# Time mixing with gate and layer norm on eight cores: unlinked transfers in the head, first products of k's mixes on ScalarE

## The chip, the cores and the metric

One Trainium2 chip, eight cores, one launch. The input x has two sequences of 4096 tokens with 2048 channels; each core computes 1024 tokens of one sequence, and reads 128 tokens before its own (the lane) so that the recurrence can start without a word from another core. The metric is the device time in microseconds of the slowest core. All trace times below are of the slowest core of one profiled execution, counted from the start of its span.

## The reference

```python
def _L0_attn_ref(x, ...):
    prev = jnp.concatenate([x[:, 1:2, :], x[:, :-1, :]], axis=1)
    xx = prev - x
    xk, xv = x + xx * tm_k, x + xx * tm_v
    xr, xg = x + xx * tm_r, x + xx * tm_g
    r, k, v = xr @ Wr.T, xk @ Wk.T, xv @ Wv.T
    g = sigmoid(xg @ Wg.T)
    w = exp(-exp(time_decay))
    wkv = _wkv_scan(k, v, w, time_first)
    o = sigmoid(r) * wkv * g @ Wo.T
    mu = o.mean(-1, keepdims=True)
    var = ((o - mu) ** 2).mean(-1, keepdims=True)
    return (o - mu) * rsqrt(var + EPS) * ln_g + ln_b

xn = _layernorm(x)
s = _L0_attn_ref(xn, ...)
g = silu(xn @ ternary(weight).T + bias)
return x + s * g
```

The scan runs over time for each channel: a = w*a + exp(k)*v, b = w*b + exp(k), with the output (a + eu*exp(k)*v) / (b + eu*exp(k)). Each mix (xr, xk, xv, xg) is tm * prev + (1 - tm) * x, one factor per channel.

## The kernel before, in words

**Layout.** Channels lie on partitions: the normalised x is `xn`, 16 slices (`ic`) of 128 channels by 1154 columns of time (f16). `mova` and `movb` hold mixes (bf16, 16 slices by 1152 columns), `att` the result of sigmoid(r) that is later multiplied by wkv and the gate. Weights come in units: a unit is 256 output channels of one matrix, in two halves of eight slices. `feed` (line 370) issues the two transfers on POOL's queue, each reading 1 MB of float32 and writing 512 KB of bf16. Units live in slots: R0, R1, R2 in a ring, X0 and X1 in space that the scan uses later. A tile of outputs is 16 products into one of eight PSUM banks, which TensorE may use again when its eviction has run (`bank_free`).

**Program order.** Each engine runs its list in the order in which the code was written; an instruction with a token waits for that count of another engine's or a transfer's semaphore, and everything behind it on its engine waits too. SP issues x and other float32 loads, POOL the weights.

**The head (lines 408 to 600).** x comes in nine blocks of 128 tokens (x1 to x8 are the core's own, x0 the lane) into four buffers `xs`. For each: statistics on DVE (`norm_stats`), normalising on ScalarE into `xh` (`norm_apply`), 16 transposes on TensorE, two copies into `xn` on DVE (`place`). Units 0 to 3 of Wr are multiplied with r's mix in pieces: 512 columns of x1 to x4, then 256 of x5 and x6, then 256 of x7 and x8. Output group j uses unit j // 2. TensorE's list in the stretch that the change touches is: groups 0 to 3 on the first 512 columns; groups 4 and 5 for slices 0 to 7 (unit 2, first half); transposes of x5; groups 4 and 5 for slices 8 to 10 (second half); transposes of x6; slices 11 to 15; then the next columns. DVE's list there is: the last mixes, statistics of x5, statistics of x6, copies of x5, copies of x6, next mixes. ScalarE's is: xh of x5, two raw evictions, xh of x6 in two pieces, two raw evictions, first products of the next mixes. r's mixes are made by `lerp_pair` (line 337): ScalarE writes (1 - tm) * x into one of four quarter buffers `lq`, DVE adds tm * prev.

**Links between the queues.** SP issues x5 and x6 when unit 1's first half has landed (`P.wait("SP", have[("wr", 1, 0)])`), x7 and x8 behind unit 2's first half, x0 behind unit 3's. POOL issues unit 2 behind x5, unit 3 behind x7, unit 4 behind unit 3's last half.

**After the head.** ScalarE makes the sigmoids that it had put off and three small Exps (line 589 on). DVE makes k's 16 mixes with `lerp` (line 325), in which both instructions are DVE's: a tensor_scalar into `lu`, one of two buffers, then a scalar_tensor_tensor. Meanwhile TensorE works through units 4 and 5 of Wr, eight tiles of 16 products in banks 4, 5, 6, 7, 0, 1, 2, 3, which ScalarE evicts with a Sigmoid (`sr_evict`, line 395). Units 6 and 7 then run slice by slice over all eight banks in the same order, so that `mova` comes free one slice at a time for v's mixes (`t_ic`). k's 16 mixes stand before v's 16 on DVE. Then k and v are computed channel block by channel block, k first; k's first product wants all of k's mixes, v's all of v's.

Of the kernel before, what the change touches and what calls it, by code (L numbers as in the profile page):

```python
# [9 lines left out]
AF = mybir.ActivationFunctionType  # L10
OP = mybir.AluOpType
# [10 lines left out]
T_ALL = LANE + T_OWN  # L22
# [3 lines left out]
TMK, TMV, TMR, TMG = 0, 1, 2, 3  # L26
# [75 lines left out]
def build_nc():  # L102
    nc = bass.Bass("TRN2", target_bir_lowering=False)
    P = Program(nc)
# [21 lines left out]
    def at(name, shape, dtype, offset):  # L126
        return nc.alloc_sbuf_tensor_at(name, shape, dtype, offset=offset)

    xn = at("xn", [128, CH, 1154], F16, XN)
    mova = at("mova", [128, CH, T_ALL], BF16, A)  # L130
    movb = at("movb", [128, CH, T_ALL], BF16, B)
# [11 lines left out]
    lu = [at("lu0", [128, T_ALL], F16, SMALL), at("lu1", [128, T_ALL], F16, ROWS + 20736)]  # L143
# [26 lines left out]
    def sm(name, n, dtype=F32):  # L170
        nonlocal small
        t = at(name, [128, n], dtype, small)
        small += -(-n * (2 if dtype == F16 else 4) // 32) * 32
        return t
    vec = sm("vec_sb", 161)
    ident = vec[:, 97:161].bitcast(F16)
    om = sm("om", 64)
# [22 lines left out]
    def next_bank():  # L200
        i = turn[0] % 8
        turn[0] += 1
        return i
# [6 lines left out]
    t_load = {}  # L210

    def load_x(b):
        i = xs_at[b]
        x_rows[b] = xs[i]
        t_load[b] = P.dma("SP", "xs%d" % i, xs[i][:, :], x_d[1 + 128 * b:129 + 128 * b, :], xs_free[i])
# [109 lines left out]
    def lerp(dst, ic, tm, col, n, *tokens):  # L325
        k = lu_n[0] % 2
        lu_n[0] += 1
        u = lu[k]
        P.op("DVE", lambda e: e.tensor_scalar(u[:, 0:n], xn[:, ic, col:col + n],
                                              om[:, 16 * tm + ic:16 * tm + ic + 1], None, OP.mult),  # L330
             *tokens)
        return P.op("DVE", lambda e: e.scalar_tensor_tensor(  # L332
            dst, xn[:, ic, col - 1:col - 1 + n], vec[:, 16 * tm + ic:16 * tm + ic + 1], u[:, 0:n],
            OP.mult, OP.add), drain=True)
# [4 lines left out]
    def lerp_pair(dst, ic, tm, col, n, *tokens):  # L339
# [9 lines left out]
            OP.mult, OP.add), t_u, *tokens)  # L349
        return lq_free[k]  # L350


    stg_free = [None] * 6
    nstg = [0]
# [7 lines left out]
    have = {}  # L362

    def feed_half(mat, u, h, slot):

        assert slot_free[slot] != "busy"
        have[(mat, u, h)] = P.dma(
            "POOL", "w%s_%d" % (slot, h),
            unit[slot][:, 8 * h:8 * h + 8, :].rearrange("p a b -> p (a b)"), w_d[mat][u, h, :, :],
            slot_free[slot])  # L370
        if h == 1:
            have[(mat, u)] = slot
            slot_free[slot] = "busy"

    def feed(mat, u, slot):
        feed_half(mat, u, 0, slot)
        feed_half(mat, u, 1, slot)
# [5 lines left out]
    def unit_tile(mat, u, oc, mov, t0, n, *tokens):  # L383

        slot = have[(mat, u)]
        b = next_bank()
        for ic in range(CH):
            tok = mm(ps[b][:, 0:n], unit[slot][:, ic, 128 * oc:128 * oc + 128],
                     mov[:, ic, t0:t0 + n], ic == 0, ic == CH - 1,
                     have[(mat, u, ic // 8)], bank_free[b], *(tokens if ic == 0 else ()),  # L390
                     signal=ic == CH - 1)
        return b, tok


    def sr_evict(b, och, t0, n, tok, c0=0):
        bank_free[b] = P.op("ACT", lambda e: e.activation(
            att[:, och, t0:t0 + n], ps[b][:, c0:c0 + n], AF.Sigmoid), tok)
# [36 lines left out]
    t_om = P.op("DVE", lambda e: e.tensor_scalar(om[:, :], vec[:, 0:64], -1.0, 1.0, OP.mult, OP.add), t_vec)  # L434
# [8 lines left out]
    P.wait("POOL", t_xh[(1, 1)])  # L443
    feed("wr", 0, "R0")
    feed("wr", 1, "R1")
    P.wait("SP", have[("wr", 1, 0)])
    load_x(5)
    load_x(6)
    P.wait("POOL", t_load[5])
    feed("wr", 2, "R2")  # L450
    P.wait("SP", have[("wr", 2, 0)])
    load_x(7)
    load_x(8)
    P.wait("POOL", t_load[7])
    feed("wr", 3, "X0")
    P.wait("POOL", have[("wr", 3, 1)])
    feed("wr", 4, "X1")


# [3 lines left out]
    def r_mm(j, ic, t0, n, bank):  # L463
        c0 = 256 if t0 == 768 else 0
        t_grp[j] = mm(ps[bank][:, c0:c0 + n],
                      unit[rslots[j // 2]][:, ic, 128 * (j % 2):128 * (j % 2) + 128],
                      mova[:, ic, t0:t0 + n], ic == 0, ic == 15,
                      have[("wr", j // 2, ic // 8)], t_ra[(t0, ic)], bank_free[bank], signal=ic == 15)
# [41 lines left out]
    for ic in range(11, 16):  # L510
        for j in (4, 5):
            r_mm(j, ic, 0, 512, j)
    P.wait("SP", have[("wr", 3, 0)])
    load_x(0)


# [75 lines left out]
    t_head = [t_xn[(0, 0)], t_xn[(0, 1)], t_xh[(0, 1)]] + xh_free  # L592
    stg_free[1] = t_grp[7]


    t_kb = [lerp(movb[:, ic, :], ic, TMK, 2, T_ALL, *t_head) for ic in range(16)]

    rslot = {3: "X0", 4: "X1", 5: "R0", 6: "R1", 7: "X0"}
    turn[0] = 4
# [3 lines left out]
    for u in (4, 5):  # L603
        for oc in range(2):
            for h in range(2):
                b, tok = unit_tile("wr", u, oc, mova, 512 * h, 512)
                sr_evict(b, 2 * u + oc, 512 * h, 512, tok)
        slot_free[rslot[u]] = tok
    kslot = [("R0", "R2", "R1")[n % 3] for n in range(16)]

# [7 lines left out]
    t_va = []  # L618
    t_ic = []
# [10 lines left out]
    t_rend = t_grp[7]  # L630

    for ic in range(16):
        t_va.append(lerp(mova[:, ic, :], ic, TMV, 2, T_ALL, t_ic[ic]))


    P.op("DVE", lambda e: e.memset(za[:, 0:1], 0.0), t_rend)
# [79 lines left out]
    for i in range(16):  # L716
        u, oc = i // 2, i % 2
        for j in range(3):
            b, tok = unit_tile("wk", u, oc, movb, 384 * j, 384, *t_kb)
# [28 lines left out]
        if i == 13:  # L748
            b = next_bank()
# [166 lines left out]
    for u in range(8):  # L916
        for oc in range(2):
            for h in range(2):
                b, tok = unit_tile("wg", u, oc, mova, 512 * h, 512, *[t_ga[ic] for ic in range(16)])
# [70 lines left out]
    for tb in range(1, NTB):  # L990
# [3 lines left out]
        for s in range(4):  # L994
            b = next_bank()
# [91 lines left out]
```

How the kernel before makes its waits and increments, by code:

```python
        def run(e):  # L60
            for s, n in todo:
                e.wait_ge(s, n)
            if drain:
                e.drain()
            ins = emit(e)
            if signal:
                ins.then_inc(self.sem[eng], 1)
# [13 lines left out]
        def run(e):  # L81
            for s, v in todo:
                e.wait_ge(s, v)
            if accum_op == OP.bypass:
                e.dma_start(out, in_).then_inc(sem, 16)
            else:
                e.dma_start(out, in_, accum_op=accum_op).then_inc(sem, 16)
# [7 lines left out]
        def run(e):  # L95
            for s, v in todo:
                e.wait_ge(s, v)
```

## Time and profile before

| what | value |
|---|---|
| median of three runs | 743.63 us (743.05 to 745.22) |
| profiled execution, its own time | 743.03 us |
| its span on the slowest core | 741.3 us (cores 739.7 to 741.3) |
| TensorE's granted clock, mean | 0.995 |
| TensorE busy | 706.4 us, 95% |
| DVE busy | 465.9 us, 63% |
| ScalarE busy | 241.3 us, 33% |
| POOL busy | 123.8 us, 17% |

The two clocks start at different points: the profiled execution took 743.03 us, its longest span 741.3 us. A timeline row shows the start, the time taken, the engine, the line of the code that recorded it (a helper's line in many cases), the operation, tile written <- tiles read and count; in brackets stands how long the engine was idle before it and what ended that. Line 380 is every product, line 290 every transpose. Weights of Wr show as wR<-wr or wX<-wr by the slot. A row of a DMA queue gives packets, MB and the busy share of 16 engines in the stretch: q0 is POOL's queue, q1 is SP's.

### The profile page before, as it was taken

The numbers are of one execution on the slowest core, as the hardware profiler recorded it, in microseconds if no ns is written. First come the engines' busy times: TensorE is split into PE (matmuls) and PEld (weight loads), VectorE is DVE, ScalarE is ACT, GpSimd is POOL, SyncE is SP. The second block draws the span as 40 slices with busy tenths as digits, with TensorE's granted clock in tenths as the row PEclk, the third lists the DMA queues.
The fourth block names the chain that finished last, engine by engine and source line by source line (L and its number), as shares of the span: only waits on it lengthen the run. The fifth ranks groups of instructions, "written<-read, shape, count | busy, mean of one in ns | idle before, by whom it ended". The sixth has DMA issues, their size and how long they took to land.

```text
span 741.3 us, 10313 instructions; the slowest of 8 cores (739.7 to 741.3 us)
## 1 busy us (share of the span) xinstructions
PE 706.4 (95%) x3809; PEld 372.0 (50%) x3852; DVE 465.9 (63%) x580; ACT 241.3 (33%) x344; POOL 123.8 (17%) x156
## 2 busy tenths in 40 slices
PE   1889999999999999999999999999999999999994
PEld 1447644456666666666665444444444444444441
DVE  6777589957777677776789496674111110566565
ACT  4766751043444234442126654412111110000000
POOL 1010101001010010100000000112134410876710
PEclk9999999999999999999999999999999999999997
DMA  8988194444783958739317933894999975356643
GB/s 237 172 222 171 30 212 85 73 114 90 195 152 95 225 117 209 144 93 217 65 51 199 334 108 78 185 168 36 138 176 149 171 149 158 86 142 156 185 113 113
DMA packets 22372, 107.71 MB, mean 145 GB/s; under 512 B 2482, under 2 KB 2610, under 8 KB 14898
## 3 DMA queue, kind: packets, MB, share of 16 engines
q0 software_dynamic: 12672, 50.34, 41.1%
q1 hardware_dynamic: 9648, 56.71, 24.5%
q8 instruction: 31, 0.51, 0.3%
q14 instruction: 17, 0.14, 0.1%
q10 hardware_dynamic: 4, 0.02, 0.0%
HBM read 140.61 MB, written 8.39 MB: 201 GB/s over the span
## 4 chain that ended last, share of the span: by engine, by line
PE 83%; DVEq 5%; DMA 5%; DVE 4%; issue 1%; ACT 1%; POOL 0%; ACTq 0%; SPq 0%; POOLq 0%
PE ps L380 83%; DVEq L64 5%; DVE movb L332 3%; DMA wR<-wr 3%; DMA xs<-x 2%; PE ps L290 1%; DVE mova L332 0%; DVE zt L966 0%; ACT xh L268 0%; DVE bst L245 0%; DVE ps L960 0%; POOL wR L85 0%; DVE xn L317 0%; ACT raw L400 0%; DVE bst L952 0%
## 5 line engine op out<-in xcount | busy, mean ns | idle before, releaser
L380 PE MATMUL ps<-mova,wR 128*128 128x384 bf16 (+2 forms) x1555 | 283.4, 340 | 5.2 <-DMA wR<-wr 3.0
L380 PEld LDWEIGHTS ps<-mova,wR 128*128 128x128 bf16 x1568 | 152.6, 98 | 130.3 <-issue 7.7
L380 PE MATMUL ps<-movb,wR 128*128 128x384 bf16 x768 | 127.4, 326 | 0.0
L380 PE MATMUL ps<-wo,att 128*128 128x512 bf16 x502 | 110.1, 379 | 0.5
L380 PE MATMUL ps<-wq,xn 128*128 128x512 bf16 x501 | 109.9, 379 | 0.7
L380 PEld LDWEIGHTS ps<-movb,wR 128*128 128x128 bf16 x768 | 75.1, 98 | 49.7
L380 PEld LDWEIGHTS ps<-wo,att 128*128 128x128 bf16 x512 | 50.1, 98 | 60.4
L380 PEld LDWEIGHTS ps<-wq,xn 128*128 128x128 f16 x512 | 50.0, 98 | 60.5 <-issue 0.3
L868 DVE TENSOR_TENSOR att<-sg,att 128x512 bf16<-128x512 bf16 x32 | 15.2, 475 | 96.1 <-ACT sg L866 96.1
L711 DVE TENSOR_TENSOR kv<-ps,ek 128x384 f32<-128x384 f32 x48 | 26.6, 557 | 51.4 <-PE ps L380 47.9
L952 DVE BATCH_NORM_STATS2 bst<-ps 128x6 f32<-128x512 f32 x32 | 21.4, 691 | 46.4 <-PE ps L380 46.4
L866 ACT ACTIVATE sg<-ps 128x512 bf16<-128x512 f32 x32 | 19.1, 597 | 87.3 <-PE ps L380 87.3
L332 DVE SCALAR_TENSOR_TENSOR mova<-xn,vec_sb,lu 128x1152 bf16<-128x1152 f16 (+2 forms) x33 | 44.0, 1333 | 3.1
L645 ACT ACTIVATE ek<-ps,hb 128x128 f32<-128x128 f32 x16 | 5.9, 367 | 120.2 <-PE ps L380 120.2
L380 PE MATMUL ps<-mova,wX 128*128 128x512 bf16 x186 | 43.9, 379 | 0.3
L657 DVE TENSOR_TENSOR_SCAN zb<-w_sb,ek 128x1152 f32<-128x1152 f32 x16 | 40.9, 2559 | 1.5
L672 DVE TENSOR_TENSOR_SCAN za<-w_sb,kv 128x1152 f32<-128x1152 f32 x16 | 40.9, 2559 | 1.4
L702 ACT ACTIVATE wq<-stg,nmag 128x2048 bf16<-128x2048 f32 x16 | 31.4, 1996 | 21.5 <-DVE stg L700 21.5
L776 DVE SCALAR_TENSOR_TENSOR ps<-ps,nscale,bias 128x512 f32<-128x512 f32 x32 | 24.2, 757 | 20.5 <-PE ps L380 19.2
L85 POOL DMA_DIRECT2D wR<-wv x16 | 8.5, 536 | 157.4 <-PE ps L380 157.4
L955 ACT ACTIVATE sd<-mv,eps 128x1 f32<-128x1 f32 x8 | 2.4, 294 | 93.4 <-DVE mv L954 93.4
L780 ACT ACTIVATE g<-ps 128x512 bf16<-128x512 f32 x32 | 18.7, 597 | 39.7 <-DVE ps L776 39.5
(83 smaller groups left out, 638.9 us busy)
## 6 DMA issues: line engine op xcount, KB each, us to landing
stg<-wf SPq DMA_DIRECT2D x32, 1024.0 KB, 9.1
xs<-x SPq DMA_DIRECT2D x9, 1024.0 KB, 9.3
wR<-wk POOLq DMA_DIRECT2D x16, 512.0 KB, 11.0
wR<-wv POOLq DMA_DIRECT2D x16, 512.0 KB, 10.7
wo<-wo POOLq DMA_DIRECT2D x16, 512.0 KB, 23.7
y<-zt SPq DMA_DIRECT2D x7, 1024.0 KB, 7.2
wR<-wg POOLq DMA_DIRECT2D x12, 512.0 KB, 17.2
stg<-x POOLq DMA_DIRECT2D x6, 1024.0 KB, 9.4
```

The costliest lines, as they stand in the source:

```text
L64: e.drain()
L332: return P.op("DVE", lambda e: e.scalar_tensor_tensor(dst, xn[:, ic, col - 1:col - 1 + n], vec[:, 16 * tm + ic:16 * tm + ic + 1], u[:, 0:n ...
L380: return P.op("PE", lambda e: e.matmul(bank, w_ap, m_ap, start=first, stop=last), *tokens, signal=signal)
L657: P.op("DVE", lambda e: e.tensor_tensor_scan(zb[:, 1:1 + T_ALL], wb, ek[m][:, :], 0.0, OP.mult, OP.add), t_weu, drain=True)
L672: P.op("DVE", lambda e: e.tensor_tensor_scan(za[:, 1:1 + T_ALL], wb, kv[:, :], 0.0, OP.mult, OP.add), drain=True)
L702: t_wq[(s, q)] = P.op("ACT", lambda e: e.activation(dst, stg[i][:, :], AF.Sign, bias=nmag[:, 0:1]), t, t_nmag, wq_free[s % 2], *tokens)
L711: bank_free[b] = P.op("DVE", lambda e, j=j, b=b: e.tensor_tensor(kv[:, 384 * j:384 * j + 384], ps[b][:, 0:384], ek[m][:, 384 * j:384 * j + ...
L776: t = P.op("DVE", lambda e: e.scalar_tensor_tensor(ps[b][:, :], ps[b][:, :], nscale[:, 0:1], bias[s % 2][:, :], OP.mult, OP.add), tok, t_b ...
L780: bank_free[b] = P.op("ACT", lambda e: e.activation(g2[s][:, tb, :], ps[b][:, :], AF.Silu), t, t_att[15] if s >= 2 else None)
L866: t = P.op("ACT", lambda e: e.activation(sg[k][:, :], ps[b][:, :], AF.Sigmoid), tok, sg_free[k])
L868: sg_free[k] = P.op("DVE", lambda e: e.tensor_tensor(att[:, och, 512 * h:512 * h + 512], sg[k][:, :], att[:, och, 512 * h:512 * h + 512], ...
L952: P.op("DVE", lambda e, s=s: e.bn_stats(bst[m][:, 6 * s:6 * s + 6], ps[banks[s]][:, :]), toks[s])
```

## The change

In the head POOL issues units 0, 1 and 2 one behind the other. SP issues x5 to x8 behind unit 1's first half. Unit 3 is issued when x6 is in, unit 4 when x8 is in. x0 waits for its buffer alone. After the head, the first product of k's mixes is made by ScalarE (`lerp_wide`), two slices before the first eviction of unit 4, and two after each eviction of units 4 and 5 until all 16 are issued; the second stays on DVE. v's mixes stay with `lerp`; the first also waits for DVE's last two readers of `lu`.

```diff
+    lw_free = [None] * 2
+
+    def lerp_wide(dst, ic, tm, *tokens):
+
+        k = ic % 2
+        t_u = P.op("ACT", lambda e: e.activation(lu[k][:, :], xn[:, ic, 2:2 + T_ALL], AF.Copy,
+                                                 scale=om[:, 16 * tm + ic:16 * tm + ic + 1]),
+                   t_om, lw_free[k], *tokens)
+        lw_free[k] = P.op("DVE", lambda e: e.scalar_tensor_tensor(
+            dst, xn[:, ic, 1:1 + T_ALL], vec[:, 16 * tm + ic:16 * tm + ic + 1], lu[k][:, :],
+            OP.mult, OP.add), t_u, *tokens)
+        return lw_free[k]
@@ -443,17 +456,13 @@
     P.wait("POOL", t_xh[(1, 1)])
     feed("wr", 0, "R0")
     feed("wr", 1, "R1")
+    feed("wr", 2, "R2")
     P.wait("SP", have[("wr", 1, 0)])
-    load_x(5)
-    load_x(6)
-    P.wait("POOL", t_load[5])
-    feed("wr", 2, "R2")
-    P.wait("SP", have[("wr", 2, 0)])
-    load_x(7)
-    load_x(8)
-    P.wait("POOL", t_load[7])
+    for b in (5, 6, 7, 8):
+        load_x(b)
+    P.wait("POOL", t_load[6])
     feed("wr", 3, "X0")
-    P.wait("POOL", have[("wr", 3, 1)])
+    P.wait("POOL", t_load[8])
     feed("wr", 4, "X1")
@@ -510,7 +519,6 @@
-    P.wait("SP", have[("wr", 3, 0)])
     load_x(0)
@@ -593,7 +601,7 @@
-    t_kb = [lerp(movb[:, ic, :], ic, TMK, 2, T_ALL, *t_head) for ic in range(16)]
+    t_kb = [lerp_wide(movb[:, ic, :], ic, TMK, *t_head) for ic in range(2)]
@@ -605,6 +613,8 @@
                 b, tok = unit_tile("wr", u, oc, mova, 512 * h, 512)
                 sr_evict(b, 2 * u + oc, 512 * h, 512, tok)
+                for ic in range(len(t_kb), min(len(t_kb) + 2, 16)):
+                    t_kb.append(lerp_wide(movb[:, ic, :], ic, TMK))
@@ -630,7 +640,7 @@
     for ic in range(16):
-        t_va.append(lerp(mova[:, ic, :], ic, TMV, 2, T_ALL, t_ic[ic]))
+        t_va.append(lerp(mova[:, ic, :], ic, TMV, 2, T_ALL, t_ic[ic], *(lw_free if ic == 0 else ())))
```

## Rows read from the trace of the kernel before

**Rows 1.** The page, parts 1 and 4: busy time, the chain by line.

```profile
PE 706.4 (95%) x3809; PEld 372.0 (50%) x3852; DVE 465.9 (63%) x580; ACT 241.3 (33%) x344; POOL 123.8 (17%) x156
...
PE ps L380 83%; DVEq L64 5%; DVE movb L332 3%; DMA wR<-wr 3%; DMA xs<-x 2%; PE ps L290 1%; DVE mova L332 0%; DVE zt L966 0%; ACT xh L268 0%; DVE bst L245 0%; DVE ps L960 0%; POOL wR L85 0%; DVE xn L317 0%; ACT raw L400 0%; DVE bst L952 0%
```

**Rows 2.** TensorE's waits: us in total, times, longest.

```profile
PE ps L380 <- DMA wR<-wr: 3.0, 2, 1.8
```

**Rows 3.** TensorE's timeline, 41 to 56 and 148 to 160 us.

```profile
46.17 3.61 PE L380 MATMUL ps<-mova,wR 128*128 128x512 bf16 x16 [1.81 <-DMA wR<-wr]
...
51.80 1.06 PE L290 MATMUL ps<-vec_sb,xh 128*128 128x128 f16 x16
52.70 2.76 PE L380 MATMUL ps<-mova,wR 128*128 128x512 bf16 x14
...
157.61 2.60 PE L380 MATMUL ps<-mova,wR 128*128 128x384 bf16 x15 [0.47 <-DVE zb L637]
```

**Rows 4.** SP's timeline at 30.7; the DMA issue at 31.3 to 31.5 (KB, us to landing).

```profile
30.70 1.22 SPq L85 DMA_DIRECT2D xs<-x  x2
...
xs<-x SPq DMA_DIRECT2D x1, 1024.0 KB, 10.3
```

**Rows 5.** Queues' packets, MB, share: 32 to 34, 34 to 42, 40 to 42, 42 to 50.

```profile
q1 hardware_dynamic: 25, 0.20, 47.1%
...
q1 hardware_dynamic: 263, 1.89, 64.7%
...
q1 hardware_dynamic: 8, 0.03, 4.0%
...
q0 software_dynamic: 287, 1.04, 80.4%
```

**Rows 6.** The same for 98 to 112 us.

```profile
q0 software_dynamic: 336, 1.25, 53.4%
q1 hardware_dynamic: 281, 2.10, 47.2%
```

**Rows 7.** Timelines of DVE and ScalarE, 41 to 55 us.

```profile
41.12 2.46 DVE L245 BATCH_NORM_STATS2 bst<-xs 128x6 f32<-128x512 f32 x4
...
44.80 2.47 DVE L245 BATCH_NORM_STATS2 bst<-xs 128x6 f32<-128x512 f32 x4
...
54.00 0.88 DVE L347 SCALAR_TENSOR_TENSOR mova<-xn,vec_sb,lu 128x256 bf16<-128x256 f16 x2 [0.19 <-ACT lu L344]
...
48.97 2.37 ACT L268 ACTIVATE xh<-xs,nm,rs 128x1024 f16<-128x1024 f32 x2 [0.67 <-DVE nm L263]
```

**Rows 8.** DVE's timeline, 124 to 128 us.

```profile
124.99 1.42 DVE L332 SCALAR_TENSOR_TENSOR movb<-xn,vec_sb,lu 128x1152 bf16<-128x1152 f16 x1
...
126.93 1.42 DVE L332 SCALAR_TENSOR_TENSOR mova<-xn,vec_sb,lu 128x1152 bf16<-128x1152 f16 x1
```

**Rows 9.** ScalarE's groups by shape (busy us, mean ns), and its timeline at 34.86.

```profile
L344 ACT ACTIVATE lu<-xn,om 128x256 f16<-128x256 f16 x32 | 13.2, 497 | 2.8 <-DVE xn L317 2.8
...
L344 ACT ACTIVATE lu<-xn,om 128x512 f16<-128x512 f16 x15 | 9.4, 709 | 3.6 <-DVE xn L317 3.6
...
34.86 5.02 ACT L344 ACTIVATE lu<-xn,om 128x512 f16<-128x512 f16 x8 [2.78 <-DVE xn L317]
```

**Rows 10.** ScalarE's timeline, 100 to 122 us.

```profile
100.60 1.28 ACT L396 ACT_TABLE_LOAD   x1
101.90 1.08 ACT L396 ACTIVATE att<-ps 128x512 bf16<-128x512 f32 x2
...
121.81 0.60 ACT L396 ACTIVATE att<-ps 128x512 bf16<-128x512 f32 x1 [2.86 <-PE ps L380]
```

**Rows 11.** Timelines of DVE and ScalarE, 398 to 420 us.

```profile
405.18 1.29 DVE L659 SCALAR_TENSOR_TENSOR ek<-ek,eu_sb,zb 128x1024 f32<-128x1024 f32 x1
...
406.56 1.07 ACT L662 ACTIVATE ek<-ek 128x1024 f32<-128x1024 f32 x1 [1.51 <-DVE ek L659]
```

**Rows 12.** TensorE's timeline, 121 to 150 us.

```profile
122.42 1.03 PE L380 MATMUL ps<-mova,wX 128*128 128x512 bf16 x4
...
149.18 7.96 PE L380 MATMUL ps<-movb,wR 128*128 128x384 bf16 x48
```

## The prediction

> **What bounds the kernel now.** I read the page first: TensorE is busy 95% of the span, and 83% of the chain that ended last is line 380, the products [rows 1]. So only TensorE's gaps can be won, and anything that opens one is lost in full. The list of waits names them: 3.0 us for Wr's transfers in two waits, the longest 1.8 us [rows 2]. TensorE's own timeline puts it in place: unit 2's first products start at 46.17 after 1.81 us of waiting; and the first product of v waits 0.47 us at 157.61 behind DVE, whose two memsets follow v's mixes [rows 3]. The change works on these two waits. If it removed both whole and opened none, it would give 1.8 + 0.5 = 2.3 us.
>
> **Part 1, the head's transfers.** Before, each link holds a transfer back until one of the other queue has landed: x5 and x6 issue from 30.70 on [rows 4], Wr unit 2 when x5 is in, near 39.7. The gaps show in the packets of the two queues: q1 (SP's, float32 copies) has moved x5 and x6 alone, 25 packets from 32 to 34 us and 263 in the next eight, only 8 of them after 40, and q0 (POOL's, which also converts to bf16) unit 2 from 42 to 50 us, 287 packets for its two halves [rows 5]. So a 1 MB block of x and a 512 KB half of a unit are 144 packets each; the work of x5 and x6 is 288, in some 7.1 us (about 33.1 to 40.2), and of unit 2 another 288, in some 6.7 us (42.0 to 48.7).
>
> After, POOL issues unit 2 right behind units 0 and 1 at about 17 to 18 us, so that its packets follow theirs at 32.3. SP still waits for unit 1's first half, so x5 to x8 issue at 30.7 as before (now four, at 0.4 us each; their buffers have long been free) and their packets start near 33. Both queues then want the same engines at once. Where that happens before, from 98 to 112 us (units 5 to 7 against wf), q0 has 336 packets at 53.4% and q1 281 at 47.2% of the engines: they halve them, 44 packets per us together, and the share of q1 lets a block through in 144 / 20 = 7.2 us [rows 6]. The Trainium skill, "DMA: Bandwidth & Descriptors", section on arbitration, says that each engine goes round-robin between the queues that it has work for; these two shares agree. It speaks against the change: the overlap that the links prevented costs each block its half, and taking the links out moves no more packets per us.
>
> - Unit 2, first half: 144 packets, the first 30 or so alone, the rest at half speed: it lands near 39. TensorE wants it at 46.17 - 1.81 = 44.36 [rows 3]. The stall of 1.81 us goes. The second half lands near 45 and is wanted after 16 products (3.61 us) and x5's transposes, at 48.8: in time.
> - x5: 33 and 7.2, with 1 for the landing, gives 41 to 43; the statistics on DVE want it at 41.12 [rows 7]. Up to 2 us late, but x5's transposes have slack up to x6's.
> - x6: work doesn't shrink. From 32.3 both queues have 288 + 288 = 576 packets to move before x6 and unit 2 are in. At 44 per us that is 13.1 us, at their separate rates 13.8: 45.4 to 46.1, and 0.9 us more until a landing is seen (x6's packets ended near 40.5 [rows 5], and it landed 10.3 us behind its issue at 31.1, at 41.4 [rows 4]). I take 46.8. DVE wants x6 at 44.80 [rows 7], so its statistics start 2.0 us late; before, x6 had been there for 3.4 us.
>
> What is late next is therefore x6. Behind its statistics on DVE stand x5's two copies; ScalarE's two pieces of xh follow them (48.97 + 2.37 = 51.34 [rows 7]) and move to 53.34; TensorE has x6's transposes in its queue ahead of unit 2's last 10 products and of everything after. By the 0.19 us that TensorE or DVE takes to start behind ScalarE [rows 7] and 8 transposes (half of 52.70 - 51.80 [rows 3]) TensorE goes on at 53.34 + 0.19 + 0.45 = 53.98 instead of 52.70: **1.3 us later**, although the wait of 1.81 us before it is gone. Bounds: x6 as early as now (41.4) leaves 51.34 + 0.64 = 51.98, a gain of 0.7 us and no more, since the statistics' chain on DVE starts only when the mixes end, at 41.1; x6 at 48.5 (one lagging engine of the 16) costs 3.0. From there TensorE's list holds no other wait for a transfer (the 3.0 us of rows 2 are both earlier), so the shift stays. x7, x8 and unit 3 come 5 us or more before their need (66.5 and later), now with SP and POOL less late; x0, moved forward to about 47.5, lands some 15 us early. These cost nothing, and their cover is that slack.
>
> **Part 2, k's mixes.** Removed: 16 tensor_scalar of 1152 columns on DVE; a mix's step falls from 1.94 us (124.99 to 126.93 [rows 8]) to one scalar_tensor_tensor (STT) of 1.42. Added: 16 ACTIVATE of 1152 columns on ScalarE, a form that the trace lacks. From 256 and 512 columns (497 and 709 ns [rows 9]) the slope is 0.83 ns a column, so 709 + 640 x 0.83 = 1.24 us each. Their step: eight of 512 take 5.02 us [rows 9], (5.02 - 0.71) / 7 = 0.616, hence 1.15 us at 1152.
>
> ScalarE's line: it ends the three Exp steps at 100.60, the load of the Sigmoid table starts there, and evictions 0 and 1 run at 101.90, already behind TensorE [rows 10]: eviction 7 starts at 121.81 after 2.86 us idle and lasts 0.60, a tile each 3.45 us, so tiles 0 and 1 were done 24.2 and 20.7 us earlier, at 97.5 and 100.9. Now two first products go ahead: 100.60 + 1.15 + 1.24 = 103.0, table load 1.28, so eviction 0 at 104.3. Then each eviction (0.52) is followed by two products (2.30): a cycle of 2.82 us. But there are two buffers: product n+2 waits for the STT of n: 1.24 + 0.19 (ScalarE to DVE) + 1.42 + 0.10 (DVE to ScalarE: 405.18 + 1.29 to 406.56 [rows 11]) = 2.95 us. The cycle is 2.95 after the first, TensorE's tile takes 3.45; ScalarE starts 7 us behind and wins back half a us a tile. Eviction 7 starts near 104.3 + 2.8 + 6 x 2.95 = 124.8 instead of 121.81 and ends at 125.4.
>
> Who waits for it: units 6 and 7 take all eight banks in turn, and the eighth product (bank 3, tile 7's) is due at 122.42 + 3 x 0.216 = 123.07 [rows 12]. TensorE would restart at 125.4 + 0.15 = 125.6: **a new wait of 2.5 us**. Bounds: 1.7 with the cycle of 2.82, 3.1 with 3.05.
>
> What the mixes win: the last STT ends with the last first product, 124.9 + 0.2 + 1.42 = 126.5, against 126.41 before [rows 8]. DVE has less work but waits for ScalarE, so v's mixes start no earlier (126.6, before 126.3) and end near 157.8. TensorE, which wanted them at 157.14 and got them at 157.61 [rows 3], now comes at 157.14 + 2.5 = 159.6 and doesn't wait. Net at this point: +2.5 - 0.5 = **+2.0 us** (bounds +1.2 and +2.6). k's mixes themselves are wanted 48 products before v's, near 149 [rows 12]. Added waits of v's first mix for lw_free are of DVE on itself: under 0.1 us, inside the chain that has slack.
>
> **Sum.** 1.3 + 2.0 = +3.3 us; both shift everything, since TensorE runs without a gap afterwards. The profiled execution (743.03 us, span 741.3) would come to 746.3, the median (743.63) to 746.9. I take 746.6.
>
> **Rivals.**
> - x6 in time: the transfers of SP's queue get through first, or x6's last packets aren't held by unit 2. For it: the packets of x5 and x6 need only 7 us alone; against: the sharing of [rows 6], where neither queue wins. Decides below 45.5 for x6's landing. Head -0.7, with part 2 +1.3: 744.6, no difference that shows.
> - ScalarE catches up: the other side, not slower. If the cycle of an eviction and two products is under 2.6 us, eviction 7 ends before 123.07, no wait opens and the 0.5 us are won. Place: bank 3 at 123. Against: the three pieces alone sum to 2.82. Price: -0.5, with the head +1.3: +0.8, 744.1; with x6 in time as well -1.2, 742.1; with nothing late at all -2.3, 741.2.
> - Table reloads: each return from a Sigmoid to a Copy loads a table, 1.28 us [rows 10], and back again: 7 x 2.57 = 18 us more on ScalarE, all of it in the wait for bank 3: about 765. For it: no row shows a Copy after a Sigmoid. Against: line 344's Copies run in the head under the table loaded for Sqrt, eight in 5.02 us [rows 9], with no load between them and the Sqrts. The Trainium skill, "ScalarE: Activation LUTs", section "Table sets: the hidden batching unit", says that cheap functions, copy among them, are in every set; no row here shows it for Sigmoid's.
> - Only one of the two losses comes: x6 much as forecast and bank 3's wait at 1.7 or less, or the reverse: +1.5 to +2.2, 745.5.
>
> **Chances.** The forecast 0.52; one loss halved 0.20; x6 in time 0.13; ScalarE catches up 0.09 and both together 0.03; reloads 0.03. Range 742.6 to 749.4: below from the rival with a small gain, above +2.6 and +3.0 together (749.2). About 0.3% (2.2 us) is what a measurement can tell. Slower by more: 0.52 and 0.03, and a few of the halved ones, 0.59. Faster by more asks for nearly every one of the 2.3 us: 0.05. Within: 0.36.
>
> **What would show it.** Right, in the profile after: no wait of TensorE for wR<-wr at 44, but x6's statistics begin near 47 behind the transfer of x, and x6's transposes wait for xh until 53; both queues with packets from 34 to 46; ScalarE's first products 1.24 us long, its eviction 7 near 126 (with the head's shift), TensorE with one wait of 2 to 3 us for ACT att near 124 to 127; no wait before the first product of v. Wrong: x6's statistics still at 44.8, TensorE at units 6 and 7 without a gap, or ACT_TABLE_LOADs between 105 and 125.

## The result and the profile after

Six runs of the changed kernel have a median of 748.32 us against 744.24 us for the kernel before on the same chips, a ratio of 1.0058 (95% interval 1.0046 to 1.0069): **slower by about 4.3 us** (0.0058 x 744.24). 746.6 was forecast, 3.0 us over the 743.63 known then. One of the six (874.79 us) fell into a slower state in which the cores of one die show a lower granted clock whatever the kernel; the ratios here leave such executions out.

The span of the slowest core grew from 741.3 to 746.2 us, and the profile's core is 6 in both. TensorE's list of waits shows both new costs, and the two that are gone are missing from it (us in total, times, longest):

```profile
...
PE ps L290 <- ACT xh L268: 9.5, 6, 2.6
PE ps L393 <- ACT att L409: 2.1, 1, 2.1
PE ps L393 <- ACT lu L344: 0.8, 1, 0.8
PE ps L393 <- DVE mova L332: 0.6, 1, 0.6
PE ps L393 <- ACT raw L413: 0.4, 2, 0.2
```

The 1.81 us for unit 2 [rows 3] are gone (of the eight cores before, only 1, 4 and 6 had such a wait, the first two with 0.76 and 1.03 us), and so is the wait for DVE's zb [rows 3]. The other wait for wR<-wr [rows 2] lies ahead of the stretch that the change touches, at the second product of the head: on this core it is the 0.8 us for lu now, on cores 0, 2 and 4 it is still there for wR<-wr with 2.28, 0.29 and 0.54 us. In their place stand 2.1 us behind an eviction of units 4 and 5 (L409) and more waiting for xh. TensorE's timeline shows where (line 393 is the old 380):

```profile
46.45 1.05 PE L290 MATMUL ps<-vec_sb,xh 128*128 128x128 f16 x16 [0.28 <-ACT xh L268]
47.34 1.46 PE L393 MATMUL ps<-mova,wR 128*128 128x512 bf16 x5
51.36 0.61 PE L290 MATMUL ps<-vec_sb,xh 128*128 128x128 f16 x8 [2.57 <-ACT xh L268]
52.49 1.01 PE L290 MATMUL ps<-vec_sb,xh 128*128 128x128 f16 x8 [0.52 <-ACT xh L268]
53.30 3.80 PE L393 MATMUL ps<-mova,wR 128*128 128x512 bf16 x14
57.28 0.27 PE L393 MATMUL ps<-mova,wR 128*128 128x256 bf16 x1 [0.19 <-ACT raw L413]
...
126.93 0.48 PE L393 MATMUL ps<-mova,wX 128*128 128x512 bf16 x1 [2.07 <-ACT att L409]
127.20 1.91 PE L393 MATMUL ps<-mova,wR 128*128 128x512 bf16 x4
128.91 1.81 PE L393 MATMUL ps<-mova,wX 128*128 128x512 bf16 x4
130.56 1.03 PE L393 MATMUL ps<-mova,wR 128*128 128x512 bf16 x4
```

x6's transposes wait 2.57 and 0.52 us; the 14 products behind them take 3.80 us where the same 14 took 2.76 [rows 3]. In units 6 and 7 the eighth product waits 2.07 us for its bank, and the two groups of four behind it take 1.91 and 1.81 us instead of 1.03. The longer times are a second price that the prediction didn't have: TensorE's granted clock fell. The table of stretches of core 0 (stretch, its length, PE's busy time and count, granted clock, DMA share, GB/s) has it behind the same wait:

```profile
122.00:124.00 2.00, 2.00 (x11) 1.00 0.00 0
124.00:126.00 2.00, 0.35 (x2) 1.00 0.00 0
126.00:128.00 2.00, 1.59 (x7) 0.91 1.04 166
128.00:130.00 2.00, 2.00 (x6) 0.50 0.99 147
130.00:132.00 2.00, 1.95 (x8) 0.74 1.08 168
132.00:134.00 2.00, 2.00 (x10) 1.00 0.85 117
```

Half clock is the lower of its two levels, 1.2 instead of 2.4 GHz. The missing shares add up to 2 x (0.09 + 0.50 + 0.26) = 1.70 us at full clock. Cores 0, 2, 3 and 6 lose 1.70 to 1.72 us so; cores 1, 4, 5 and 7 have the same 2.06 us of waiting and lose nothing. Core 6 alone also had a fall near 52 us, behind its wait of 2.57 us, and core 0 one at 32 to 36 us, behind a wait of 2.28 us for wR<-wr. The one on core 0 cost nothing: its first product on the columns of x5 and x6 comes 10.19 us behind the start of x6's statistics, as in the kernel before on the same core.

Why x6's transposes waited is on DVE, as forecast in kind: on this core the statistics of x5 and of x6 now wait for their transfers, and those of x6 start at 45.98 instead of 44.80 [rows 7]:

```profile
40.26 2.47 DVE L245 BATCH_NORM_STATS2 bst<-xs 128x6 f32<-128x512 f32 x4 [0.34 <-DMA xs<-x]
...
45.98 2.47 DVE L245 BATCH_NORM_STATS2 bst<-xs 128x6 f32<-128x512 f32 x4 [1.98 <-DMA xs<-x]
```

On the other cores x6's statistics don't wait for the transfer itself, but start behind x5's, which waited for theirs on six of those seven. When x6 was in can be read there too: POOL issues unit 3 when x6 has landed, and on the four cores of this kernel and of e1 where DVE waits for x6, POOL is 0.44 us behind DVE. By that, x6 was in at 46.0 to 47.0 us on cores 0, 2, 5, 6 and 7 and at 43.4 to 44.0 on cores 1, 3 and 4.

The two queues' packets of core 4 from 34 to 36 us show the sharing (packets, MB, share); in the kernel before q1 had such a stretch for itself [rows 5]:

```profile
q1 hardware_dynamic: 42, 0.34, 48.4%
q0 software_dynamic: 42, 0.16, 45.7%
```

ScalarE's timeline on core 6 is the one forecast, cycle for cycle, 1.5 us later because the head ended later:

```profile
102.13 2.40 ACT L357 ACTIVATE lu<-xn,om 128x1152 f16<-128x1152 f16 x2
104.54 1.28 ACT L409 ACT_TABLE_LOAD   x1
105.84 0.60 ACT L409 ACTIVATE att<-ps 128x512 bf16<-128x512 f32 x1
106.33 2.39 ACT L357 ACTIVATE lu<-xn,om 128x1152 f16<-128x1152 f16 x2
108.62 0.58 ACT L409 ACTIVATE att<-ps 128x512 bf16<-128x512 f32 x1
...
123.81 2.49 ACT L357 ACTIVATE lu<-xn,om 128x1152 f16<-128x1152 f16 x2
126.21 0.57 ACT L409 ACTIVATE att<-ps 128x512 bf16<-128x512 f32 x1
```

From eviction 1 to eviction 7 are (126.21 - 108.62) / 6 = 2.93 us each; there is one table load for Sigmoid and none between Copies and Sigmoids.

### The profile page after: what moved, and what is told of

The parts are those of the page before. It is cut to its first block, busy times and chain, and to the rows that moved or that the text cites. A ratio compares the mean times of both kernels' runs of the same rounds, so it can differ in the third digit from the quotient of the medians.

```text
span 746.2 us, 10327 instructions; the slowest of 8 cores (741.2 to 746.2 us)
## 1 busy us (share of the span) xinstructions
PE 709.1 (95%) x3809; PEld 372.5 (50%) x3852; DVE 460.2 (62%) x564; ACT 259.7 (35%) x360; POOL 123.3 (17%) x156
## 4 chain that ended last, share of the span: by engine, by line
PE 87%; ACT 4%; DMA 4%; issue 2%; DVE 1%; DVEq 0%; SPq 0%; ACTq 0%
PE ps L393 87%; DMA xs<-x 4%; ACT lu L357 1%; ACT xh L268 1%; PE ps L290 1%; ACT att L416 1%; ACT att L409 0%; DVEq L64 0%; SPq L85 0%; DVE zt L976 0%; ACT lu L344 0%; DVE bst L245 0%; DVE ps L970 0%; ACT L597 0%; ACT xn L315 0%
## 5 line engine op out<-in xcount | busy, mean ns | idle before, releaser
L878 DVE TENSOR_TENSOR att<-sg,att 128x512 bf16<-128x512 bf16 x32 | 16.8, 524 | 94.1 <-ACT sg L876 94.1
L962 DVE BATCH_NORM_STATS2 bst<-ps 128x6 f32<-128x512 f32 x32 | 21.4, 693 | 46.8 <-PE ps L393 46.8
L290 PE MATMUL ps<-vec_sb,xh 128*128 128x128 f16 (+1 forms) x160 | 13.2, 245 | 20.8 <-DMA vec_sb<-vec 11.2
```

The lines of the kernel that those rows point to most:

```text
L290: t_tr[(b, h)] = P.op("PE", lambda e, ic=ic, c=c, view=view: e.transpose(view[:, n * c:n * c + n], xh[s][0:n, 128 * ic:128 * ic + 128], id ...
L878: sg_free[k] = P.op("DVE", lambda e: e.tensor_tensor(att[:, och, 512 * h:512 * h + 512], sg[k][:, :], att[:, och, 512 * h:512 * h + 512], ...
L962: P.op("DVE", lambda e, s=s: e.bn_stats(bst[m][:, 6 * s:6 * s + 6], ps[banks[s]][:, :]), toks[s])
```

## Experiments

All with a ratio are from five rounds against the kernel before on the same chip. "Head" below is the stretch from TensorE's first product to its first product on the columns of x5 and x6; before, it takes 25.7 to 26.4 us on the eight cores (median 25.9).

**e1, the head's part alone.** The transfers as changed, k's mixes as before.

> Only the transfers of the head are changed; k's mixes are as before. Theory (x6 comes late because unit 2 shares the engines with it): the statistics of x6 wait for its transfer until about 46 to 47, TensorE waits for xh of x6 near 51, and the first product on the columns of x5 and x6 starts 1 to 1.7 us later than before, 2 us more where the clock falls behind the wait; the whole +1 to +2 us. The wait of 0.47 us before v's first product stays. Rival (the head gains and all the loss is made by k's mixes): -0.5 to -1.5 us.

Measured: 1.0021 (1.0010 to 1.0032), +1.6 us. The head takes 25.9 to 28.9 us, median 27.4. v's first product waits 0.49 us as before. Both blocks are late. On DVE, x6's statistics follow x5's; on core 4, the slowest (743.4 us):

```profile
43.81 2.48 DVE L245 BATCH_NORM_STATS2 bst<-xs 128x6 f32<-128x512 f32 x4 [2.83 <-DMA xs<-x]
...
47.49 2.47 DVE L245 BATCH_NORM_STATS2 bst<-xs 128x6 f32<-128x512 f32 x4
...
47.21 1.06 POOL L85 DMA_DIRECT2D wX<-wr  x2 [28.26 <-DMA xs<-x]
```

x5 is not ready until 43.8; x6's statistics start right behind x5's chain, without a wait for x6 itself. Seven of the eight cores wait for x5, three for x6. But x6 was hardly earlier: POOL's issue of unit 3, less the 0.44 us, puts it at 46.8 on this core, 0.7 us ahead of its statistics, and at most 0.3 us ahead of them on the others. So the late x6 alone would have cost nearly as much, and x5's lateness adds up to 0.7 us. No clock fell behind these waits (core 6 had a fall at 32 to 38 us, behind a wait of 1.97 us for lu, which cost nothing, as in the changed kernel's core 0). The rival (the head gains) is out.

**e2, the mixes' part alone.**

> Only k's mixes are changed; the transfers of the head are as before. Theory (ScalarE is behind by more than it can win back, eviction 7 holds bank 3): TensorE waits 2.07 us for that eviction as in the changed kernel, v's wait of 0.47 us goes, net +1.6 us, and up to 1.8 us more on cores where the granted clock is at 0.5 behind the wait; +2 to +3.4 us. Rival (ScalarE was late only because the head's transfers delayed it): the wait is under 0.5 us and the kernel gains 0.3 to 0.5 us. If both parts add up, this one and the head's sum to about +4.1 us.

Measured: 1.0029 (1.0017 to 1.0042), +2.2 us. All eight cores wait 2.06 to 2.08 us for bank 3, whatever their head did, so ScalarE's delay doesn't come from the transfers. Six of the eight lose 1.70 to 1.72 us of clock behind it (core 0 as much near 34 us instead, behind a wait of 2.12 us for wR<-wr); core 5, by stretches:

```profile
120.00:122.00 2.00, 1.93 (x9) 1.00 0.00 0
122.00:124.00 2.00, 0.00 (x0) 1.00 0.74 121
124.00:126.00 2.00, 2.00 (x7) 0.69 1.02 203
126.00:128.00 2.00, 2.00 (x7) 0.50 1.08 217
128.00:130.00 2.00, 2.00 (x10) 0.96 1.06 160
```

e1 and e2 add to 0.0050, the changed kernel has 0.0058, and the intervals are +-0.0012 each: within them the two parts add up.

**e3, the eighth bank's products later.** As e2, with another order in units 6 and 7:

```diff
-        for j, (u, oc, h) in enumerate(tiles):
...
+        todo = [(ic, j) for j in range(7)] if ic < 3 else [(ic, j) for j in range(8)]
+        if ic == 2:
+            todo += [(0, 7), (1, 7), (2, 7)]
+        for c, j in todo:
+            u, oc, h = tiles[j]
...
```

> As the one with only k's mixes changed, but in units 6 and 7 the eighth bank's products of the first three slices run behind the other seven banks' of these slices, so that TensorE has 3 us of other products while eviction 7 is made. Theory (the loss of the mixes is this one wait and the clock behind it): the wait of 2.07 us is gone, no stretch at clock 0.5 near 125 to 131, and the time is that of before within 0.5 us, 1.6 to 3.4 us less than with only the mixes changed; v's mixes on DVE still end near 158 and TensorE waits for them by 0 to 0.6 us. Rival (ScalarE's backlog costs elsewhere too, by the later evictions or by the start of k): the time stays over +1 us.

Measured: 0.9998 (0.9988 to 1.0009). The wait for att is gone on every core, and so is the fall of the clock. Core 6's remaining wait behind DVE is v's:

```profile
PE ps L393 <- DMA wR<-wr: 2.6, 2, 1.5
PE ps L393 <- DVE zb L657: 0.8, 1, 0.8
```

0.8 us instead of 0.5, because v's mixes now wait for the first slice (t_ic) that this order frees later. So ScalarE's backlog cost nothing but this one wait and the clock behind it, and moving k's first products to ScalarE, with that repaired, wins nothing that these runs can tell.

**e6, a short wait.** As e3 with two slices instead of three held back, so that 7 products lie ahead of the wait instead of 14.

> Only k's mixes are changed, and in units 6 and 7 the eighth bank's products of two slices, not three, run behind the other banks': 7 products (1.51 us) more than in the changed kernel lie ahead of the wait for eviction 7. Theory (the wait itself is the loss, and the fall of the clock comes with a wait of 2 us): a wait of 0.55 us is left, no stretch at clock 0.5, v's first product waits near 0.2 us; +0.1 to +0.5 us over before. Rival (any wait there lowers the clock): 1.7 us of clock lost on six or so of the eight cores, +2 us.

Measured: 1.0001 (0.9990 to 1.0011). Of its profile only cores 4 to 7 are read (mean granted clock 0.994 to 0.997; cores 0 to 3 had 0.948 to 0.984). Each of the four waits 0.55 to 0.56 us at the bank and none has a stretch below 1.00. Core 4, by stretches:

```profile
120.00:122.00 2.00, 2.00 (x11) 1.00 0.12 18
122.00:124.00 2.00, 1.45 (x8) 1.00 0.92 178
124.00:126.00 2.00, 1.95 (x10) 1.00 1.12 223
126.00:128.00 2.00, 2.00 (x11) 1.00 1.06 203
```

Waits of 2.07 us were followed by a fall on 10 of 16 cores (e2 and the changed kernel), waits of 0.55 us on none of four. v's first product doesn't wait on these cores, which I had put at 0.2 us.

**e4, only half a unit ahead.** The head again; k's mixes as before:

```diff
+    feed_half("wr", 2, 0, "R2")
     P.wait("SP", have[("wr", 1, 0)])
     load_x(5)
     load_x(6)
     P.wait("POOL", t_load[5])
-    feed("wr", 2, "R2")
-    P.wait("SP", have[("wr", 2, 0)])
+    feed_half("wr", 2, 1, "R2")
+    P.wait("SP", t_load[6])
```

> The head again, k's mixes as before: only the first half of Wr's unit 2 goes right behind unit 1; its second half is issued when x5 has landed, x7 and x8 when x6 has. Theory (packets of both queues share the engines half and half, and x6 is late by the packets of unit 2 that run beside it): 144 packets beside x5 and x6 instead of 288, 432 in all, so x6 lands near 43 to 44 and is in time for 44.8; unit 2's first half lands near 39, the wait of up to 1.8 us for it is gone; gain 0.3 to 0.8 us on the cores that had that wait, nothing on the others; the whole -0.8 to 0 us. Rival (any packets of POOL's queue beside x hold x back by its first packets, whatever their number): x6 near 46 again and +1 us.

Measured: 0.9988 (0.9979 to 0.9997), -0.9 us, the lowest ratio of all. The head takes 25.7 to 26.0 us on every core; the longest of the kernel before was 26.35, so the head of its profile accounts for 0.35 of the 0.9. On core 4, the slowest (741.7 us), x5's statistics start with the end of the mixes and x6's right behind:

```profile
41.95 0.15 DVE L490 TENSOR_SCALAR hb<-vec_sb 128x1 f32<-128x1 f32 x1
42.02 2.47 DVE L245 BATCH_NORM_STATS2 bst<-xs 128x6 f32<-128x512 f32 x4
...
45.69 2.47 DVE L245 BATCH_NORM_STATS2 bst<-xs 128x6 f32<-128x512 f32 x4
```

Its timeline of TensorE still has 0.27 and 0.52 us of waiting for xh at x6's transposes: the bound of the prediction, by which no more than 0.7 us can be won here however early x comes (the rows below). Half of the rival is seen: x5's first packets come 3.7 to 4.3 us after the issue on seven cores (2.8 on core 7), as late as with all of unit 2 ahead, against 1.0 to 2.4 in the kernel before. Its price isn't: x is in time all the same, so the number of packets beside it decides.

```profile
51.37 0.61 PE L290 MATMUL ps<-vec_sb,xh 128*128 128x128 f16 x8 [0.27 <-ACT xh L268]
52.50 0.61 PE L290 MATMUL ps<-vec_sb,xh 128*128 128x128 f16 x8 [0.52 <-ACT xh L268]
```

**e5, x7 and x8 not in the queue.** Unit 2 whole behind unit 1, but `P.wait("SP", t_load[6])` ahead of x7 and x8.

> The head with unit 2 right behind unit 1, but only x5 and x6 issued behind unit 1's first half; x7 and x8 wait for x6; k's mixes as before. Theory (unit 2's packets beside x5 and x6 are what makes x late): the same as with all four blocks issued, x5's statistics wait for their transfer up to 43 on most cores, +1 to +2 us. Rival (four blocks in SP's queue hold each other back): x5 and x6 come in time for 41 and 45, the wait for unit 2 is gone, -0.8 to 0 us.

Measured: 1.0014 (1.0005 to 1.0023), +1.0 us. x5's statistics wait 0.24 to 1.6 us on six of eight cores, and the head's median is 26.7 us. Unit 2's packets alone make x late. Whether x7 and x8 add something (0.0014 here against 0.0021 in e1) the intervals leave open, and the profiles can't tell: SP's first packets come at 32.4 to 34.5 us here and at 33.1 to 35.6 in e1, because x5 was issued earlier here (28.2 to 30.4 against 29.0 to 31.7), and that moves x5 as much.

**e7, half of k's first products on ScalarE.** The head as before. DVE makes three of k's mixes alone at once, then the engines alternate:

```diff
+    for ic in range(3):
+        k_dve(ic, *t_head)
...
+                for n in range(2):
+                    if len(t_kb) < 16:
+                        if n == 0:
+                            t_kb.append(lerp_wide(movb[:, len(t_kb), :], len(t_kb), TMK))
+                        else:
+                            k_dve(len(t_kb))
```

> The head as before. k's first three mixes are DVE's alone, as soon as the head is done; then each eviction of units 4 and 5 is followed by one first product on ScalarE and one mix of DVE alone. Theory (ScalarE at 0.5 + 1.15 us a tile of 3.45 catches up, DVE is freed by some 4 us): no wait at bank 3, v's mixes end before v's first product wants them, the wait of 0.49 us goes: -0.5 us. Rival (v's mixes are held by the slices of mova that TensorE frees, so that freeing DVE moves nothing): the wait of 0.49 us stays, 0 us.

Measured: 0.9995 (0.9986 to 1.0004). The wait before v's first product is gone on all cores (v's mixes end 1.4 us ahead of it on core 2), but a wait at bank 3 of 0.25 us is left:

```profile
PE ps L391 <- ACT att L407: 0.3, 1, 0.3
```

DVE, not ScalarE, paces this version: a lone mix and an STT take 3.27 us of a tile's 3.45, and ScalarE, idle 1.53 us in each cycle, stands with its next first product ahead of the eviction. The net of 0.49 - 0.25 = 0.24 us is below what these runs can tell; both the theory and its rival fit the ratio. The trace decides for the theory where the two differ, at v's first product; the theory's other claim, no wait at bank 3, was wrong by the 0.25 us.

**e8, both repaired.** e4 and e7 together.

> The head with only the first half of unit 2 ahead, together with half of k's first products on ScalarE. Theory (both parts work on separate waits): -0.9 us from the head's version and -0.5 us from the mixes', -1.0 to -1.4 us, a ratio of 0.998. Rival (the gains share one chain): no more than the better of the two, -0.9 us.

Measured: 0.9992 (0.9983 to 1.0000), -0.6 us. Its profile has neither the wait for v nor one over 0.26 us at bank 3, and a head of 25.7 to 25.9 us; on core 0 the second half of unit 2 is 0.40 us late. That it is no better than e4 alone (0.9988) is within the intervals; of the forecast of -1.0 to -1.4 us only the smaller end lies within this one, and the gain of both over one isn't shown.

## Why the prediction was right, and what it missed

- **The removed waits.** Right: the wait of 1.81 us for unit 2 and that of 0.47 us before v are both gone.
- **Part 1: x late by the sharing of the engines.** Right in mechanism, shown by e1 (late), e5 (late without x7 and x8) and e4 (144 packets less beside x, in time). The even shares of both queues, which the prediction took from [rows 6], came back as 48.4% and 45.7%, with 42 packets each; the Trainium skill ("DMA: Bandwidth & Descriptors", Arbitration) says that each engine takes the queues that it has work for in turn, packet by packet, and this trace agrees. "I take 46.8" for x6's landing met 46.0 to 47.0 on five cores; on cores 1, 3 and 4, where x5 was issued at 28.1 to 28.7 us, x6 was in near 44 and its statistics start as before. Two things in it were wrong and hardly show in the time. The packets of x5 don't "start near 33": the prediction took 2.4 us from issue to first packet, as in the kernel before, where POOL has nothing queued behind unit 1; with unit 2 queued it is about 4 us, and on the four cores of the changed kernel with an issue near 31 they start at 34.7 to 35.4. x6's forecast didn't hang on that start, since it counted the packets of both queues and q0 moved its own meanwhile; x5's did. And what the prediction called x5's slack was none, since x6's statistics stand behind x5's on DVE; because x6 was itself in so late, this adds 0.7 us at most. The size, +1.3 us, was measured as +1.6 (e1), whose interval is 0.7 to 2.4.
- **Part 2: ScalarE's cycle.** Right step by step: a first product of 1.24 us (measured 2.40 for two overlapped), a cycle of 2.95 (2.93), eviction 7 near 126 (126.21). The wait, forecast as 2.5 us, shows as 2.07. Of the difference, 0.16 is only a way of counting: the prediction counts from the moment at which the product was due (124.05 + 3 x 0.216 = 124.70), the profile from the end of the product before it (124.86). TensorE came 1.63 us later than before and ScalarE 1.53, which is 0.10, and 0.15 is ScalarE's (the cycles and a shorter eviction). No reloads of tables: that rival was out, and this trace agrees with what the Trainium skill ("ScalarE: Activation LUTs", "Table sets: the hidden batching unit") says of Copy, here beside Sigmoid.
- **The missed term: the clock.** The working took each wait at its own length. Behind 2.07 us of waiting the clock went to 0.5 and cost 1.7 us more on four cores of the profile. The sum without it is 1.6 (e1) + 2.07 - 0.49 = 3.2 us. On the profile's core 6 it is there twice and gives the whole growth of the span, 4.9 us: 1.63 at the start of units 6 and 7 (of it 1.04 from the fall near 52 us), 2.07 of waiting, 1.70 of clock, less 0.47 at v. Measured over the executions were 4.3 us, and 2.2 for e2, whose sum is 1.6 without the fall and 3.3 with it. Both lie between because the time is that of the slowest of eight cores. An estimate from the spans: without the falls core 7 would end last in the changed kernel's profile, at 744.4 instead of 746.2 us, a price of 1.8; in e2's it would be core 4, which had none, at 744.5 instead of 744.6, a price of 0.1. The last core's mean granted clock is 0.990 to 0.993 in all five executions that count for the changed kernel, against 0.993 to 0.997 for the kernel before in the experiments' rounds, which suggests a fall in most of them; a count from traces wasn't made.
- **Part 2 had nothing to win.** Right: k's STTs end with ScalarE's last first product, so v's mixes start no earlier (128.02 on core 6, 126.4 without the head's shift). e7 shows that the wait of 0.49 us can be had only when ScalarE takes less.
- **What was luck.** The forecast of +3.0 stands near the 3.2 us that the waits come to. That 748.32 us lies in its range is no merit of its working: the range was drawn for a later x6 and a longer wait at bank 3, and the clock isn't in it. Of its totals most start from 743.3 us, but 749.2 from 743.63, and 743.3 - 2.3 is 741.0 where it has 741.2; neither changes the outcome.

## What to carry to other kernels

A link that holds back one queue's transfer can protect the other's: before removing it, count the packets that both have to move before the earliest need, and let only those ahead that are wanted first. Work put in front of an eviction costs nothing until the bank is wanted again; add up the line of the engine that evicts, the wait for the second buffer included, from its backlog at the start to that bank. And a wait of 2 us on TensorE can cost nearly twice its length, since the clock may fall behind it.

## What the runs showed of the hardware

- Between 27 and 730 us the granted clock fell to 0.5 in fourteen places of the profiles (cores 0 to 3 of e6 left out), each behind a wait of TensorE of 1.97 to 2.57 us and each for 1.70 to 1.72 us of lost time. Six other waits of 2.06 to 2.08 us, on other cores of the same executions, had no fall, and neither had any wait of 1.93 us or less (1.93, 1.87, 1.83 and twice 1.81 are the longest). What decides it isn't settled here. A fall in front of a later wait can cost nothing, as on core 0 of the changed kernel.
- With more of POOL's packets queued, SP's first packets come later after their issue: 3.7 to 4.5 us on 31 of the 32 cores of the changed kernel, e1, e4 and e5, against 1.0 to 2.4 us in the kernel before, where unit 2 wasn't issued yet. It is as long with one half of unit 2 ahead (e4) as with both. The cause was not tried.
- The eight cores' first products start up to 2.6 us apart (27.4 to 29.9 us in e7's profile), more than most versions here win or lose; differences of versions have to be read within a core, from a common point.
